# A block of two layers with routed experts: the shared second layer by channels, the residual added by VectorE, and the first weight copies issued earlier

## The reference

```python
x = _layernorm(x + attn(x))                 # attn: layer norms, time mixing, the wkv scan, channel mixing
ys = _geglu(xf @ Ws1 + bs1) @ Ws2 + bs2     # shared expert, hidden width 256
top_val, top_idx = jax.lax.top_k((xf @ Wr + br) / 1.5, 2)
h = einsum('nd,edh->enh', xf, We1) + be1    # 12 experts, hidden width 384
yE = einsum('enh,ehd->end', _geglu(h), We2) + be2
yr = einsum('end,ne->nd', yE, w)            # w: softmax of the two chosen logits
x = _layernorm(x + ys + yr)
```

## Time and profile before

| | |
|---|---|
| median of 3 runs | 470.45 us |
| the profiled execution's own time | 469.14 us |
| its span, first to last instruction | 467.4 us |
| mean granted TensorE clock | 0.961 |
| PE busy | 405.8 us (87%) |
| DVE / ACT / POOL busy | 313.4 / 273.0 / 271.0 us |

### The profile page before, as it was taken

One profiled execution on the slowest core, in us unless ns is written; L12 is line 12 of the kernel. 1 busy time (PEld: TensorE's weight loads), 2 busy tenths in 40 slices (PEclk: granted clock), 3 DMA queues, 4 the chain that ended last, 5 costly groups with the idle time before them and its releaser, 6 DMA issues.

```text
span 467.4 us, 9975 instructions
## 1 busy us (share of the span) xinstructions
PE 405.8 (87%) x2658; PEld 321.1 (69%) x2658; DVE 313.4 (67%) x1057; ACT 273.0 (58%) x648; POOL 271.0 (58%) x360
## 2 busy tenths in 40 slices
PE   0176799998989897999998698999999999999991
PEld 0133466765655583877666698999999999999530
DVE  4669889999999999644831555555655555655162
ACT  2476599998978766595532354455545555554055
POOL 4766757586567867788777543444444444444264
PEclk9997789999999898999999599999999999999997
DMA  5389900000001000111132566666666666764393
GB/s 153 90 169 356 280 1 0 1 1 2 0 2 42 24 31 14 44 37 48 61 108 67 181 225 222 233 232 241 243 233 239 228 230 231 249 234 174 120 325 113
DMA packets 49261, 64.09 MB, mean 137 GB/s; under 512 B 9916, under 2 KB 32188, under 8 KB 49208
## 3 DMA queue, kind: packets, MB, share of 16 engines
q1 hardware_dynamic: 44760, 54.08, 34.8%
q0 software_dynamic: 4448, 9.38, 6.0%
HBM read 20.87 MB, written 13.91 MB: 74 GB/s over the span
## 4 chain that ended last, share of the span: by engine, by line
PE 54%; DVE 12%; POOL 12%; issue 9%; DMA 5%; ACT 4%; SPq 2%; ACTq 0%; DVEq 0%; POOLq 0%
PE bank L1244 23%; PE bank L1262 11%; POOL dispatched_rows L407 7%; PE bank L956 4%; PE bank L974 4%; PE bank L907 2%; PE bank L908 2%; DVE bst L478 2%; PE bank L1236 2%; PE bank L985 1%; DMA xnT_all<-routed_rows 1%; PE bank L986 1%; POOL rstd L817 1%; POOL frs L817 1%; ACT z L683 1%
## 5 line engine op out<-in xcount | busy, mean ns | idle before, releaser
L1133 POOL DMA_INDIRECT routed_rows<-yo,goes_to x75 | 71.8, 958 | 102.3 <-DVE yo L1172 99.6
L1244 PE MATMUL bank<-xT,w 128*128 128x128 f32 x900 | 119.6, 284 | 5.8 <-DMA w<-we_sb 3.9
L1244 PEld LDWEIGHTS bank<-xT,w 128*128 128x128 f32 x900 | 108.9, 195 | 8.3 <-issue 5.8
L1208 ACT ACTIVATE gl<-bank,tile_bias 128x128 f32<-128x128 f32 x225 | 66.7, 365 | 60.3 <-PE bank L1244 59.3
L1165 DVE SCALAR_TENSOR_TENSOR actT<-bank,tile_bias,gl 128x128 f32<-128x128 f32 x225 | 65.7, 345 | 31.4 <-PE bank L1244 25.4
L407 POOL DMA_INDIRECT dispatched_rows<-rows_all,slot_i x64 | 64.2, 1003 | 18.5 <-issue 17.3
L1262 PE MATMUL bank<-we_sb,actT 128*128 x450 | 62.7, 276 | 1.0 <-DVE yo L1172 0.9
L1262 PEld LDWEIGHTS bank<-we_sb,actT 128*128 128x128 f32 x450 | 56.1, 192 | 1.4 <-issue 1.4
L1172 DVE TENSOR_SCALAR yo<-bank,goes 128x128 f32<-128x128 f32 x75 | 26.3, 350 | 33.6 <-PE bank L1231 33.4
L956 PE MATMUL bank<-xk,wfk_sb 128*128 128x512 f32 x64 | 34.2, 649 | 5.2 <-DVE xk L575 4.2
L1202 ACT ACTIVATE xT<-bank 128x128 f32<-128x128 f32 x75 | 20.8, 277 | 28.9 <-PE bank L1236 28.2
(11 more groups left out here) (204 smaller groups left out, 824.2 us busy)
## 6 DMA issues: line engine op xcount, KB each, us to landing
w<-we_sb SPq DMA_DIRECT2D x75, 384.0 KB, 2.7
x_all<-dispatched_rows SPq DMA_DIRECT2D x75, 68.0 KB, 2.0
we_sb<-we SPq DMA_DIRECT2D x1, 4608.0 KB
rows_all<-x SPq DMA_DIRECT2D x8, 256.0 KB, 2.7
x_all<-routed_rows SPq DMA_DIRECT2D x8, 256.0 KB, 4.8
xnT_all<-routed_rows SPq DMA_DIRECT2D x8, 256.0 KB, 6.6
out<-x_all SPq DMA_DIRECT2D x8, 256.0 KB, 2.3
routed_rows<-yo,goes_to POOLq DMA_INDIRECT x75
```

What stands on the lines that cost most here:

```text
L1133: ng.indirect_dma_start(routed, bass.IndirectOffsetOnAxis(ap=goes_to[n // U % DB][:, n % U:n % U + 1], axis=0), yo[n % YO][:, :], None).th ...
L1208: na.activation(gl[n % 2][:, j * P:(j + 1) * P], ps_g[j][:, 0:P], ACT.Gelu, bias=tile_bias[:, HK + j, n:n + 1]).then_inc(s2["gelu_ready"], 1)
L1244: return nt.matmul(to[:, 0:P], w1[m][:, off:off + P], xT[m][:, :], start=True, stop=True)
```

## The change

The shared second layer now takes Ws2 as the stationary operand, two matmuls of 512 columns a chunk, so its result has channels on the partitions. VectorE's new `shared_take` adds bank, bias (a column per partition) and `xnT_all`, in place in `xnT_all`. GpSimd's additions are gone, and so are the bias matmuls of the shared layer and three small transfers for it. In the last stage TensorE turns `xnT_all` back while it adds it (`add_turned`), and `y_second` is loaded into `x_all`, whose tokens lie 544 bytes apart, and no longer into `xnT_all`. SP issues the first five weight copies as soon as the tiles are known, ahead of its wait for the dispatch; from tile 5 on its order is rows n, weights n.

```diff
-        y_second = xnT_all[:, :].rearrange("p (n c) -> p n c", c=C)
+        y_second = x_all
...
+            def shared_take(c):
+                if c == 0:
+                    v.wait_ge(s["bias_loaded"], 2 * 16)
+                v.wait_ge(s2["sh_out"], c + 1)
+                at = slice(c * W, (c + 1) * W)
+                nv.scalar_tensor_tensor(xnT_all[:, at], sh_y[:, :], bs2_col, xnT_all[:, at], ALU.add, ALU.add).then_inc(s2["sh_taken"], 1)
...
+            shared_act(1, 0); placed(v, 2, pT[:, PT_PREFIX]); x3(7); shared_act(1, 1); stats3(7)
+            shared_take(0); logits(6); shared_act(2, 0); shared_act(2, 1); logits(7); chosen(v, 3)
+            shared_take(1); shared_act(3, 0); shared_act(3, 1); placed(v, 3, pT[:, PT_PREFIX]); shared_take(2)
+            find_tiles(); shared_act(4, 0); shared_act(4, 1); tell_tiles(); shared_take(3); shared_act(5, 0)
+            shared_act(5, 1); shared_take(4); shared_act(6, 0); shared_act(6, 1); shared_take(5)
+            shared_act(7, 0); shared_act(7, 1); shared_take(6); shared_take(7)
...
             def shared_back(c):
                 if c == 0:
-                    t.wait_ge(s2["shared_rows_moved"], 3 * 16)
                     t.wait_ge(s["x1_ready"], CH)
                 t.wait_ge(s2["sh_act"], (c + 1) * HS)
                 after2(t, "sh_taken", c)
-                for n in range(CT):
-                    for j in range(HS):
-                        nt.matmul(sh_y[:, n * P:(n + 1) * P], ash[:, j, n * P:(n + 1) * P], ws2_sb[:, j, :],
-                                  start=j == 0, stop=False)
-                    last = biased(sh_y[:, n * P:(n + 1) * P], BS2, C)
+                for j in range(HS):
+                    last = nt.matmul(sh_y[:, :], ws2_sb[:, j, :], ash[:, j, :], start=j == 0, stop=j == HS - 1)
                 last.then_inc(s2["sh_out"], 1)
...
+            sp.wait_ge(s2["tiles_known"], 1)
+            for n in range(U):
+                load_weights(n)
+            sp.wait_ge(s["dispatched"], SLOTS // P * 16)
+            sp.wait_ge(s2["pads_placed"], E * 16)
             for n in range(U):
                 load_rows(n)
-            for n in range(TILES):
+            for n in range(U, TILES):
+                load_rows(n)
                 load_weights(n)
-                if n + U < TILES:
-                    load_rows(n + U)
...
-            g.wait_ge(s["dispatched"], SLOTS // P * 16)
-            for c in range(CH):
-                at = slice(c * CT, (c + 1) * CT)
-                g.wait_ge(s2["sh_taken"], c + 1)
-                ng.tensor_tensor(x_all[:, at, :], x_all[:, at, :], shared_out[:, at, :], ALU.add).then_inc(s2["sh_added"], 1)
...
+            def add_turned(c):
+                for n in range(CT):
+                    at = slice(n * P, (n + 1) * P)
+                    nt.matmul(banks[c][:, at], xnT_all[:, c * W + n * P:c * W + (n + 1) * P], ident[:, :], start=n == 0, stop=False)
```

More of the change, by code:

```diff
@@ L81, in build @@
         we2_sb = sb("we2_sb", [P, E, HK, C])
-        BE2, BS2 = 0, E * C
         sq_sb = sb("sq_sb", [P, 5, C])
@@ L197, in build @@
         block_buffers.close()
-        bias_rows = sb("bias_rows", [P, E * C + C], BF16)
+        bias_rows = sb("bias_rows", [P, E * C], BF16)
         run_i = sb("run_i", [P, E], I32)
@@ L258, in build @@
         s2 = {}
-        for n in ("rows_moved shared_rows_moved rows_known pads_placed tiles_known tiles_step "
+        for n in ("rows_moved rows_known pads_placed tiles_known tiles_step "
                   "word_psum code_psum code_ready bias_psum bias_ready owner_ready own_ready goes_step goes_ready "
-                  "sh_gate sh_up sh_gelu sh_act sh_out sh_taken sh_added "
+                  "sh_gate sh_up sh_gelu sh_act sh_out sh_taken "
                   "xT_psum xT_ready gate_ready up_ready gelu_ready act_ready y_ready yo_ready "
@@ L282, in gate_bank @@
             return pkv if j and c >= EARLY else pv
-        shared_out = xnT_all[:, :].rearrange("p (n c) -> p n c", c=C)
+        bs2_col = braw[:, B2:NB]
         fin = [banks[c][:, :].rearrange("p (n c) -> p n c", c=C) for c in range(CH)]
@@ L773, in shared_gelu @@
                 na.activation(gsh[:, j, :], gate_bank(c, j)[:, :], ACT.Gelu, bias=col(BS1 + HS + j)).then_inc(s2["sh_gelu"], 1)
-            def shared_take(c):
-                a.wait_ge(s2["sh_out"], c + 1)
-                na.activation(shared_out[:, c * CT:(c + 1) * CT, :], sh_y[:, :].rearrange("p (n c) -> p n c", c=C), ACT.Copy).then_inc(s2["sh_taken"], 1)
             def take_biases():
@@ L804, in attention_scalar @@
             relu(7, 1); square(7, 1); relu(7, 2); square(7, 2); relu(7, 3); square(7, 3); norm3(6)
[L805 to L809, removed]
+            shared_gelu(1, 1); gate2(7); by_channel(6); shared_gelu(2, 0); shared_gelu(2, 1)
+            norm3(7); by_channel(7); shared_gelu(3, 0); shared_gelu(3, 1); fallen(a, 3)
+            shared_gelu(4, 0); shared_gelu(4, 1); shared_gelu(5, 0)
+            shared_gelu(5, 1); shared_gelu(6, 0); shared_gelu(6, 1)
+            shared_gelu(7, 0); shared_gelu(7, 1); take_biases()
         def over_deviation(g, ve, nm, rs, nmr_, mv_, step, c, ready):
@@ L987, in rwkv @@
                 last.then_inc(s["po_ready"], 1)
-            def biased(to, row, width):
-                return nt.matmul(to, ones_bf[:, :], bias_rows[:, ds(row, width)], start=False, stop=True)
             def bank_read(c, j, of, first, other):
@@ L1074, in experts_sync @@
             sp.wait_ge(s["split"], 5)
-            for lo, hi, base, name in ((B2, NB, BS2, "shared_rows_moved"), (0, B2, BE2, "rows_moved")):
-                for n in range(3):
-                    sp.dma_start(bias_rows[n:n + 1, base:base + (hi - lo) * P], bpart[n][:, lo:hi]).then_inc(s2[name], 16)
+            for n in range(3):
+                sp.dma_start(bias_rows[n:n + 1, :], bpart[n][:, 0:B2]).then_inc(s2["rows_moved"], 16)
             sp.wait_ge(s2["rows_known"], 1)
@@ L1082, in experts_sync @@
                 sp.dma_start(dispatch[ds(to, P), :], pad_rows[n * P:(n + 1) * P, :]).then_inc(s2["pads_placed"], 16)
-            sp.wait_ge(s2["tiles_known"], 1)
-            sp.wait_ge(s["dispatched"], SLOTS // P * 16)
-            sp.wait_ge(s2["pads_placed"], E * 16)
             def load_rows(n):
@@ L1100, in load_weights @@
                 sp.dma_start(w1[n % U][:, :], we1_sb[:, ds(e, 1), :].rearrange("p a h -> p (a h)")).then_inc(w1_loaded[n % U], 16)
+            sp.wait_ge(s2["tiles_known"], 1)
[3 more added lines that the diff above has]
+            sp.wait_ge(s2["pads_placed"], E * 16)
             for n in range(U):
                 load_rows(n)
-            for n in range(TILES):
+            for n in range(U, TILES):
+                load_rows(n)
                 load_weights(n)
-                if n + U < TILES:
-                    load_rows(n + U)
             for m in range(YO):
                 sp.wait_ge(scattered[m], len(range(m, TILES, YO)) * 16)
-            sp.wait_ge(s2["sh_added"], CH)
             for c in range(CH):
@@ L1263, in second @@
                               we2_sb[:, ds(e, 1), j, :].rearrange("p a c -> p (a c)"), start=j == 0, stop=False)
-                biased(ps_y[:, 0:C], BE2 + e * C, C).then_inc(s2["y_ready"], 1)
+                biased(ps_y[:, 0:C], e * C, C).then_inc(s2["y_ready"], 1)
             t.wait_ge(s2["owner_ready"], 1)
@@ L1287, in experts_tensor, with add_to @@
             second((TILES - 1) % UA, TILES - 1, e[U])
-            def add_to(c, of, first=False, last=False):
-                return nt.matmul(banks[c][:, :], ident[:, :], of[:, c * CT:(c + 1) * CT, :], start=first, stop=last)
-            t.wait_ge(s2["sh_added"], CH)
+            def add_to(c, of, last=False):
+                return nt.matmul(banks[c][:, :], ident[:, :], of[:, c * CT:(c + 1) * CT, :], start=False, stop=last)
+            def add_turned(c):
+                for n in range(CT):
+                    at = slice(n * P, (n + 1) * P)
+                    nt.matmul(banks[c][:, at], xnT_all[:, c * W + n * P:c * W + (n + 1) * P], ident[:, :], start=n == 0, stop=False)
             t.wait_ge(s2["gelu_ready"], TILES * HK)
@@ L1296, in experts_tensor @@
             for c in range(CH - 1):
-                add_to(c, x_all, first=True)
+                add_turned(c)
             t.wait_ge(s2["yo_ready"], TILES)
-            add_to(CH - 1, x_all, first=True)
+            add_turned(CH - 1)
             for c in range(CH):
```

## The result

The changed kernel takes 543.28 us, the median of 4 runs (542.39 to 548.48), against 470.11 before (4 runs, 469.33 to 470.94): a ratio of 1.1579, 95% interval 1.1503 to 1.1655. The forecast was 533, with a range of 507 to 552. The profiled execution took 542.39 us with a span of 540.7; before it was 469.14 and 467.4.

The account below looks back on a forecast made before the run. The prediction took TensorE to bound the kernel nearly throughout the tile stretch, with transfers ahead of it. 469.14 + 51.8 - 3.6 + 17.9 - 2.5 + 0.9 = 533.6, stated as 533 us, range 507 to 552.

Parts of the forecast that it names:

- SP's order: Tile loop: rows m+7 queue behind weights waiting for up m+1, stalling TensorE at 14 calls; +51.8 us, less 3.6.
- What was added for late products and for SP: Tile loop, per call: 0.5 us for products following one by one, 0.3 because SP cannot make up late issues.
- the hole at tile 9: Kernel before, between tile 9's gate and up matmuls: TensorE idles 1.42 us for VectorE, which waited for a row transfer.
- SP always stands at that wait, not behind its own issue work: Tile loop: with five weight copies in hand, SP always waits for up matmuls; weights m+6 go at about s+1.6.
- longer stalls: Tile loop: row transfers behind a 384 KB copy land after 3.6 us instead of 2.0; +22 us, 556 us; chance 0.09.
- The clock: Tile loop: TensorE's clock falls to half after 8 of 10 holes, 1.6 us each; +17.9 us, between 0 and 28.
- the clock holds: Tile loop: same stalls, but TensorE stays at 2.4 GHz; 516 us; chance 0.20.
- The start: Start of the tiles: without GpSimd's additions beside where_to(0), the first product comes at 260.6 to 261.6; -2.5 us.
- the working on the shared layer: Shared layer: fewer matmuls and VectorE's additions, none on the chain between 251.56 and 261.67; 0 us, between -1 and +1.5.
- The last stage: Last stage: y_second in 512-byte pieces loads slower, 290 against 393 GB/s, by chunk 3; +0.9 us, between 0 and +2.
- The sum: Whole kernel: all terms added to the profiled 469.14 us give 533.6 us, 13% slower.

Follow-up runs that it names:

- where_to_one_later: The changed kernel with where_to called one tile later (n = 5k+3 instead of 5k+2); 493.79 us, ratio 1.0472 to the kernel before.
- late_rows_on_before: The kernel before, shared layer and last stage kept, with only SP's new order: five early weight copies, rows n behind weights n-1; 541.58 us, ratio 1.1486.
- takes_in_gaps: Changed kernel with row transfers back in front of the weights and each shared_take from chunk 1 on between the next chunk's two activations; ratio 0.9898.
- changed_again: The changed kernel as it is, run again beside other kernels on the same chip; 542.21 us, ratio 1.1524 to the kernel before.
- second_in_2kb_again: Second run of the changed kernel with rows ahead of weights, shared_take between the next chunk's activations, y_second in 2 KB pieces; 463.69 us, ratio 0.9851.

## Why the prediction was right, and where it was off

- **SP's order.** Right in place, mechanism and size. `other` waits 14 times in the loop, the row transfer leaves 1.08 us behind the weights that wait for the tile's matmuls, the holes come every fifth tile. Without the low clock the loop grew by 70.4 - 22.1 = 48.3 us, where 51.8 - 3.6 = 48.2 was expected; 44.8 of it is idle time. That it fits to 0.1 us is luck. The holes were longer than worked out, 46.5 / 14 = 3.3 us instead of 2.9: four of them 3.4 to 4.6, the rest 2.9 to 3.4. What was added for late products and for SP, 0.8 us a call, was too much by about as much, although the working took the hole at tile 9 as 1.6 us where the row has 1.42. "SP always stands at that wait, not behind its own issue work" fails in the first two calls. The rival "longer stalls", a row transfer that lands late, holds for two of the fourteen. And VectorE's waits were to be 2 to 4 us each; they were 4.2 to 5.9; in the call shown VectorE was ready 0.65 us after the start of tile m+1. The two kernels that change SP's order alone, in either direction, leave no other cause for it.
- **The clock: the term that was mis-sized.** "A fall at 8 of 10 calls: 14 x 0.8 x 1.6 = +17.9". Falls: 11 of 14, as taken. The price of one was taken from a single low stretch of 3 us; seven lasted about as long, 3.4 us, but four lasted 6.8. On matmuls they cost 23.0 us, 2.1 a fall, and 22.1 against the kernel before: inside the bounds of 0 to 28 and 4.2 over the term. This is the loop's distance from the forecast: 70.4 against 66.1.
- **The rival "the clock holds"** falls: it gave 516 us, and where_to_one_later shows what such a kernel looks like, with no fall at holes of up to 2.4 us.
- **The start: the step that failed.** "-2.5, between -4 and -0.5", counted to the first product, measured +1.6: 265.33 instead of 263.76. Right were that the early copies free tile 0 of its wait for weights (late_rows_on_before starts it 2.8 us earlier) and that the instructions of `where_to(0)` take 0.17 us once no additions of GpSimd run beside them. Two steps were off. SP was later than thought: the padding began at 234.30, 3.0 us later than before, and rows 0 went out at 256.36 instead of 254.5 to 255, so `where_to(0)` began at 262.06 instead of 259.8 to 260.8. By this alone the first product would have come at about 262.8 (262.06 + 0.73, an estimate), a gain of 1.0. The rest is the working on the shared layer. It named the one wait behind `shared_take(1)`, with 0.6 us of cover, and gave it at most 1.5 us. There are four such waits, 8.4 us, and the last one, at 257.36, stands directly ahead of the biases and tile 0, on the chain. The cost came from the chain of before, "none of it is on the chain": true of the kernel before, but the change puts TensorE's queue behind VectorE's there, and the first product now waits 2.48 us for TensorE. Placing the additions in VectorE's gaps takes all these waits away (takes_in_gaps).
- **The last stage.** +0.9 forecast, +1.3 measured; over the kernels with 512-byte pieces the stage took 31.3 to 32.5 us, over those with the old last stage 30.8 to 31.4, so the forecast is within what repeats. In changed_again, the same kernel, it took 31.5, only 0.3 more than before. The wait is where it was expected: TensorE waits 1.3 us for `rows_all` from `routed_rows`, against 0.55 before, and in second_in_2kb_again not at all. `add_turned` was put at 0 and costs 0.3 us: 7.36 for its 64 matmuls, against 7.09 for the 16 before.
- **The sum**, 533.6, came out 8.8 us under the profiled 542.39: 4.3 from the loop, 4.1 from the start, 0.4 from the last stage. The median lies 0.9 above that execution.

## What to carry to other kernels

An in-order DMA queue is a dependency: before moving a transfer behind another, ask what that other waits for, and whether the engine it waits for stands behind the first one's consumer. A loop through two queues then costs in every round, here 3.3 us of TensorE at every fifth tile, and in this TensorE-bound loop the low clock behind the holes added almost half to the price again: 22.1 us to 48.3. A change with several parts needs each part timed alone: the order of one queue cost 15% here, and the rest, with that order, the place of the additions and the size of the pieces mended, gains 1.5%.

## What the runs showed of the hardware

- After idle holes of 2.9 to 4.6 us TensorE's granted clock fell from 1.00 to 0.50 (2.4 to 1.2 GHz) in 11 of 14 cases, for 3.4 or 6.8 us, beginning between 1.4 us before the work returned and 1.8 us after. Which of the two lengths follows is not explained by the length of the hole: 3.06 and 3.08 us were followed by the long one, 3.94 and 4.24 by the short one. The four long ones are those that began earliest, 0.7 to 1.4 us before the work returned. Behind the holes of where_to_one_later, 2.4 us at most, it did not fall.
- 2.4 us of matmuls whose result nobody reads, put into each hole, cut the falls from 11 to 3 and the time from 542.2 to 533.7 us.
- Row transfers of 68 KB issued one at a time behind a 384 KB copy landed after 1.8 to 2.0 us at 12 of the 14 calls and after 3.2 and 3.5 us at two; in the filled kernel five took 2.7 to 4.0 us.
- One chip took 27.9 us or more for the 12 padding transfers that took 15.1 on others, and the kernel before took 496 us on it instead of 470.
- Instructions of VectorE on 10 elements a partition took 1.20 us beside GpSimd's additions of 128x512, and 0.17 without them.
